# A fused attention and quantised-MLP block on one core: both batches' attention steps issued in one piece

## The reference

```python
x = x + fake_quant(layernorm(x)) @ fake_quant(ctx)          # ctx 2 x 2048 x 2048, 8-bit steps
x = x + attention(layernorm(x), Wq, Wkv, Wo)                # 32 heads of 64, one shared key/value head
x = x + layernorm(x) @ W4 + bias                            # W4: 4-bit weights, scales per 128 rows

# attention: q = h @ Wq; k, v = split(h @ Wkv)
scores = einsum('bqhd,bkd->bhqk', q, k) / 8 + slope[h] * (k_pos - q_pos), masked above the diagonal
out = einsum('bhqk,bkd->bqhd', softmax(scores), v) @ Wo
```

## Time and profile before

| | us |
|---|---|
| median of 3 runs | 397.14 (396.98 to 397.20) |
| profiled execution | 397.71 |
| its span in the trace | 395.9 |
| TensorE busy | 354.6 (90%) |
| VectorE busy | 328.7 (83%) |
| ScalarE busy | 221.7 (56%) |

### The profile page before, as it was taken

The page is one execution under the profiler, slowest core; times in us unless marked ns, Lnnn a source line. Parts: engine busy times, 40 slices in busy tenths (PEclk is TensorE's granted clock), DMA queues, the critical chain, the costliest instruction groups (busy, mean ns, idle before and its releaser), DMA issues.

```text
span 395.9 us, 5717 instructions
## 1 busy us (share of the span) xinstructions
PE 354.6 (90%) x2342; PEld 265.2 (67%) x2342; DVE 328.7 (83%) x333; ACT 221.7 (56%) x316; POOL 29.8 (8%) x69
## 2 busy tenths in 40 slices
PE   0076865899999999999999999999999999999996
PEld 0022231425888787888877888888888788888884
DVE  1689889797879898884999967888988999999924
ACT  1788988997515872845856570742834923333100
POOL 6000000006590000000011000000000000000000
PEclk9999889699999999999999999999999999999999
DMA  8999999999055487496539624786000020000006
GB/s 333 422 436 424 428 434 427 427 397 395 17 212 170 152 208 218 118 216 208 206 111 269 208 99 165 260 309 223 2 0 1 2 106 2 0 0 2 0 0 212
DMA packets 21958, 77.37 MB, mean 195 GB/s; under 512 B 1354, under 2 KB 1402, under 8 KB 18810
## 3 DMA queue, kind: packets, MB, share of 16 engines
q1 hardware_dynamic: 21924, 77.01, 53.5%
q10 hardware_dynamic: 8, 0.00, 0.0%
HBM read 74.91 MB, written 2.10 MB: 194 GB/s over the span
## 4 chain that ended last, share of the span: by engine, by line
PE 72%; DVE 19%; DMA 4%; issue 3%; ACT 1%; ACTq 0%; DVEq 0%
PE bank L1189 22%; PE bank L1049 11%; PE bank L1050 11%; PE bank L1051 11%; DVE q L708 7%; PE bank L1010 4%; DMA raw<-in_L_attn_Wq 3%; PE bank L1062 2%; DVE stats L622 2%; PE bank L1042 2%; PE bank L1134 2%; DMA prm_row<-in_L_xattn_x_zp 2%; PE bank L1072 1%; PE bank L1153 1%; DVE resid L720 1%
## 5 line engine op out<-in xcount | busy, mean ns | idle before, releaser
L486 ACT ACTIVATE w_hi<-raw 128x2048 fp32r<-128x2048 f32 x29 | 55.2, 1912 | 44.3 <-DMA raw<-in_L_attn_Wo 22.6
L652 DVE TENSOR_TENSOR w_lo<-raw,w_hi 128x2048 fp32r<-128x2048 f32 x27 | 62.6, 2326 | 12.7 <-ACT w_hi L486 12.7
L1189 PE MATMUL bank<-w_hi,hd 128*128 128x512 f32 x208 | 53.2, 391 | 0.1
L1010 PE MATMUL bank<-q,at 128*128 128x512 bf16 x128 | 38.4, 429 | 16.1 <-DVE q L708 15.5
L1189 PEld LDWEIGHTS bank<-w_hi,hd 128*128 128x128 f32 x208 | 38.8, 188 | 8.5 <-issue 0.5
L708 DVE TENSOR_SCALAR q<-q 128x2048 bf16<-128x2048 uint8 x32 | 38.4, 1218 | 4.7 <-PE bank L1017 4.3
L1049 PE MATMUL bank<-w_hi,hd 128*128 128x512 f32 x104 | 40.7, 391 | 0.0
L1050 PE MATMUL bank<-w_lo,hd 128*128 128x512 f32 x104 | 40.5, 389 | 0.0
L1051 PE MATMUL bank<-w_hi,hd 128*128 128x512 f32 x104 | 40.5, 389 | 0.0
L1049 PE MATMUL bank<-w_hi,xt 128*128 128x512 f32 x96 | 38.9, 405 | 0.0
L1050 PE MATMUL bank<-w_lo,xt 128*128 128x512 f32 x96 | 37.5, 390 | 0.0
(11 more groups left out here) (158 smaller groups left out, 616.7 us busy)
## 6 DMA issues: line engine op xcount, KB each, us to landing
raw<-in_ctx SPq DMA_DIRECT2D x8, 2048.0 KB, 15.3
raw<-in_L_attn_Wq SPq DMA_DIRECT2D x16, 1024.0 KB, 6.0
ctx_more<-in_ctx SPq DMA_DIRECT2D x7, 2048.0 KB, 16.1
raw<-in_L_attn_Wo SPq DMA_DIRECT2D x13, 1024.0 KB, 5.1
raw_fifth<-in_L_attn_Wo SPq DMA_DIRECT2D x3, 1024.0 KB, 5.1
resid<-in_x SPq DMA_DIRECT2D x2, 1024.0 KB, 12.6
ctx_more<-in_ctx SPq DMA_DIRECT2D x2, 1024.0 KB, 15.3
scale<-in_L_ffn_scales SPq DMA_DIRECT2D x16, 128.0 KB, 6.7
```

What stands on the lines that cost most here:

```text
L486: nc.scalar.activation(hi_slots[s], raw_slots[s], ACT.Copy).then_inc(w_hi_set, 1)
L652: nc.vector.tensor_tensor(lo_slots[s], raw_slots[s], hi_slots[s].bitcast(F32), ALU.subtract).then_inc(w_lo_set, 1)
L1010: mm(bank[:, 4 * b + n, :], at[:, k, b * P:(b + 1) * P], q16[:, i % 2, n * CH:(n + 1) * CH], start=start, stop=False)
L1189: return mm(bank[:, 4 * b + n, :], left[:, j, b * P:(b + 1) * P], right[slot_of(W_F + j)][:, n * CH:(n + 1) * CH], start=part == 0 and j = ...
```

## The change

1. The scores of both batches of a group are made in one piece, `scores(g)`, in all 512 columns of banks 4 to 7. It waits for the query transpositions of both batches. It stands where the first batch's scores stood.
2. `attend(g)` makes the heads of both batches in one piece, in columns 0 to 255 of the same banks, over scores that VectorE has read. It stands where the second batch's piece stood.
3. `heads_hi(g)` and `heads_lo(g)` split both batches' output in one instruction each, of twice the width.
4. ScalarE does the exponentials of both batches one behind the other, and then the upper parts of the next two weight pieces. VectorE does both batches' biased scores and maxima, then one remainder, then both batches' divisions and transpositions, then two remainders.
5. The values go out of PSUM by one copy into `v_rows`; `v_rep` is made from it by 8 copies on VectorE and 8 on ScalarE. ScalarE's piece 6 and its 8 copies come before the loading of the exponential's table.
6. `o_granule(5, 0)` comes before `o_granule(3, 0)`.

```diff
+        v_rows = sb("v_rows", [P, B, DH], F32)
...
-            return bank[:, BLOCK_BANK:BLOCK_BANK + 4, (2 + b) * P:(3 + b) * P]
+        HEADS_AT = bank[:, BLOCK_BANK:BLOCK_BANK + 4, 0:B * P]
...
+            def heads_hi(g):
+                act.wait_ge(av_done, g + 1)
+                nc.scalar.activation(hd_hi[:, 4 * g:4 * g + 4, :], HEADS_AT, ACT.Copy).then_inc(hi_out, B)
...
+            upper_w(6)
+            act.wait_ge(v_out, 1)
+            for j in range(4):
+                for i in range(2, 4):
+                    nc.scalar.activation(v_rep[BLK * i:BLK * i + BLK, :, j, :], v_rows[BLK * j:BLK * j + BLK],
+                                         ACT.Copy).then_inc(v_dup_act, 1)
             nc.scalar.activation(warm[:], eps_col[:], ACT.Exp)
-            upper_w(6)
...
                 upper_w(4 * n + 3)
                 exps(ua)
+                exps(ub)
                 upper_w(4 * n + 4)
-                exps(ub)
-                heads_hi(ua)
                 upper_w(4 * n + 5)
-                heads_hi(ub)
+                heads_hi(n - 1)
...
-                    dve.wait_ge(score_done, u - 1)
+                    dve.wait_ge(score_done, n)
...
+            nc.vector.tensor_copy(v_rows[:], bank[:, KV_BANK, B * P:B * P + B * DH].rearrange("p (b d) -> p b d", b=B)
+                                  ).then_inc(v_out, 1)
+            q_blocks(1)
+            dve.wait_ge(v_out, 1)
             for j in range(4):
-                for i in range(4):
+                for i in range(2):
...
-                dve.wait_ge(score_done, u + 1)
+                dve.wait_ge(score_done, u // B + 1)
...
-                    dve.wait_ge(av_done, u - 1)
+                    dve.wait_ge(av_done, u // B)
...
+            def heads_lo(g):
+                dve.wait_ge(hi_out, 4 * B + B * (g + 1))
+                nc.vector.tensor_tensor(hd_lo[:, 4 * g:4 * g + 4, :], HEADS_AT, hd_hi[:, 4 * g:4 * g + 4, :].bitcast(F32),
+                                        ALU.subtract).then_inc(lo_out, B)
...
-                remainder_w(4 * n + 3)
                 biased_scores(ub)
                 maxima(ub)
+                remainder_w(4 * n + 3)
                 over_sum(ua)
                 prob_blocks(ua)
-                remainder_w(4 * n + 4)
                 over_sum(ub)
                 prob_blocks(ub)
-                heads_lo(ua)
+                remainder_w(4 * n + 4)
                 remainder_w(4 * n + 5)
-                heads_lo(ub)
+                heads_lo(n - 1)
...
+            def scores(g):
+                pe.wait_ge(qt_set, B * (g + 1))
+                if g == 0:
+                    pe.wait_ge(v_out, 1)
+                    pe.wait_ge(k_dup, 8)
                 else:
+                    pe.wait_ge(lo_out, 4 * B + B * g)
+                for b in range(B):
...
+            def attend(g):
+                if g == 0:
+                    pe.wait_ge(v_dup, 8)
+                    pe.wait_ge(v_dup_act, 8)
+                pe.wait_ge(score_out, B * (g + 1))
+                for b in range(B):
+                    probs = prob_t[:, b, :].rearrange("p (e i j q) -> p e j i q", e=2, i=4, j=4)
+                    pe.wait_ge(prob_t_set, B * g + b + 1)
...
                 if n >= 2:
-                    scores(ua)
+                    scores(n - 1)
                 q_granule(w, 1)
                 if n == 1:
-                    scores(ua)
+                    scores(n - 1)
                 q_granule(w + 1, 0)
-                scores(ub)
                 q_granule(w + 1, 1)
                 q_granule(w + 2, 0)
                 q_granule(w + 2, 1)
-                attend(ua)
                 q_granule(w + 3, 0)
                 if n >= 2:
-                    attend(ub)
+                    attend(n - 1)
                 q_granule(w + 3, 1)
                 if n == 1:
-                    attend(ub)
+                    attend(n - 1)
...
             o_granule(4, 0)
-            attend(7)
+            attend(3)
             o_granule(4, 1)
+            o_granule(5, 0)
             o_granule(3, 0)
-            o_granule(5, 0)
             o_granule(3, 1)
```

More of the change, by code:

```diff
@@ L197, in perceiver @@
         v_dup = sem("v_dup")
+        v_dup_act = sem("v_dup_act")
+        v_out = sem("v_out")
         stored = sem("stored")
@@ L276, in perceiver @@
         O_BANK = ((0, 1), (2, 3), (0, 1), (6, 7))
-        def heads_at(b):
-            return bank[:, BLOCK_BANK:BLOCK_BANK + 4, (2 + b) * P:(3 + b) * P]
+        HEADS_AT = bank[:, BLOCK_BANK:BLOCK_BANK + 4, 0:B * P]
         def tr_bank(n, g):
@@ L806, in _ @@
             dve.wait_ge(vt_done, 1)
-            values = bank[:, KV_BANK, B * P:B * P + B * DH].rearrange("p (b d) -> p b d", b=B)
+            nc.vector.tensor_copy(v_rows[:], bank[:, KV_BANK, B * P:B * P + B * DH].rearrange("p (b d) -> p b d", b=B)
+                                  ).then_inc(v_out, 1)
+            q_blocks(1)
+            dve.wait_ge(v_out, 1)
             for j in range(4):
-                for i in range(4):
+                for i in range(2):
                     nc.vector.tensor_copy(v_rep[BLK * i:BLK * i + BLK, :, j, :],
-                                          values[BLK * j:BLK * j + BLK]).then_inc(v_dup, 1)
-            q_blocks(1)
+                                          v_rows[BLK * j:BLK * j + BLK]).then_inc(v_dup, 1)
             def lower_scales(h):
@@ L829, in biased_scores @@
                                                          scalar=slope[:, u // B, e:e + 1],
-                                                         in1=bank[:, BLOCK_BANK:BLOCK_BANK + 4, e * P:(e + 1) * P],
+                                                         in1=bank[:, BLOCK_BANK:BLOCK_BANK + 4,
+                                                                  (2 * (u % B) + e) * P:(2 * (u % B) + e + 1) * P],
                                                          op0=ALU.mult, op1=ALU.add)
@@ L1115, in value_rows @@
                 ins.then_inc(vt_done, 1)
[L1117 to L1124, removed]
+            def scores(g):
+                pe.wait_ge(qt_set, B * (g + 1))
+                if g == 0:
+                    pe.wait_ge(v_out, 1)
                     pe.wait_ge(k_dup, 8)
                 else:
[L1127 to L1135, removed]
-                ins.then_inc(score_done, 1)
@@ new lines, in scores @@
+                for b in range(B):
+                    heads = qt[:, b, :].rearrange("p (e c m) -> p e c m", e=2, c=2)
+                    for e in range(2):
+                        for c in range(2):
+                            for i in range(4):
+                                rows = slice(BLK * i, BLK * i + BLK)
+                                ins = mm(bank[:, BLOCK_BANK + i, (2 * b + e) * P:(2 * b + e + 1) * P], heads[rows, e, c],
+                                         k_rep[rows, b, c, :], start=c == 0, stop=c == 1)
@@ new lines, in scores @@
+                ins.then_inc(score_done, 1)
+            def attend(g):
[6 more added lines that the diff above has]
+                    pe.wait_ge(prob_t_set, B * g + b + 1)
+                    for j in range(4):
+                        for e in range(2):
+                            for r in range(4):
+                                rows = slice(BLK * r, BLK * r + BLK)
+                                ins = mm(bank[e * DH:(e + 1) * DH, BLOCK_BANK + r, b * P + BLK * j:(b + 1) * P],
+                                         v_rep[rows, b, j, :], probs[rows, e, j, j:], start=j == 0, stop=j == 3)
@@ L1282, in _ @@
                 q_granule(w + 2, 1)
-                attend(ua)
                 q_granule(w + 3, 0)
                 if n >= 2:
-                    attend(ub)
+                    attend(n - 1)
                 q_granule(w + 3, 1)
                 if n == 1:
-                    attend(ub)
+                    attend(n - 1)
             o_granule(0, 0)
-            scores(6)
+            scores(3)
             o_granule(0, 1)
             o_granule(1, 0)
-            scores(7)
             o_granule(1, 1)
@@ L1299, in _ @@
             o_granule(2, 1)
-            attend(6)
             o_granule(4, 0)
-            attend(7)
+            attend(3)
             o_granule(4, 1)
+            o_granule(5, 0)
             o_granule(3, 0)
-            o_granule(5, 0)
             o_granule(3, 1)
```

## The result

| | before | after |
|---|---|---|
| median, us (5 runs each) | 397.14 (396.87 to 397.20) | 394.95 (394.89 to 395.11) |
| profiled execution, us | 397.71 | 394.95 |
| its span, us | 395.9 | 393.1 |
| from the first query granule of round 1 to the product behind the last `attend` | 104.80 | 102.27 |

The ratio is 0.9947 (95% interval 0.9932 to 0.9961), 2.2 us less. The profiled execution of before was 0.6 us above its median, that of after is the median, so the two traces differ by 2.8. Of these, 0.26 lie ahead of the attention: the first query granule starts at 125.60 before and 125.34 after, with no edit there (in the eleven traces of the changed kernel and its variants this start lies between 125.23 and 125.82, so 0.26 is within what executions differ by).

The account below looks back on a forecast made before the run. TensorE bounds the kernel from about 126 us. Six merges x 0.37 = 2.2, plus 0.32 wait, less 0.07: about 2.5 us off 397.71, 395.2; that execution being 0.6 above median, 394.7. Range 393.9 to 396.8.

Parts of the forecast that it names:

- The bound: From about 126 us to the end TensorE sets the time; work moved on VectorE or ScalarE alone is worth nothing.
- A merge: Second batch's scores or attend following in the same TensorE pass saves 0.37 or 0.36 us; eight merges.
- edges-only rival: Each merge on TensorE saves only the 0.21 us seen at piece edges: 1.2 us less, 396.0; chance 0.18.
- rival of no saving: A merge saves nothing because each batch fills anew: 0.5 us more, 397.6; chance 0.08.
- The new wait: Round 1, second scores: TensorE waits some 0.8 us for both batches' remainders and query transpositions, with one granule as cover.
- 0.04 to the subtraction: Round 1, chain to the second scores: 0.04 us from ScalarE's copy to VectorE's heads subtraction.
- The old wait: Round 3: TensorE's 0.32 us wait for `hd_lo` ahead of the second attention product goes.
- Margins of round 1: VectorE's roundings and probabilities in round 1 are all in time for TensorE, by 0.7 to 1.5 us.
- Value copies: Before round 1's first scores and exponentials: the split copies on VectorE and ScalarE cost nothing, being covered by TensorE's work.
- Round 3: Probabilities, hanging on weight 14's landing at 182.9, ready at 199.7; TensorE at `attend(2)` at 200.2, 0.5 us in hand.
- slower rival: Round 3: weight 14 landing after 184.2 delays TensorE at `attend(2)`; 6 us late gives 399.4; chance 0.07.
- Behind the attention: VectorE's chain after the attention moves along with TensorE; if it stayed put it would take back 0.5 us.

Follow-up runs that it names:

- the cut pieces: Changed kernel with seven of eight merged pieces cut in two by three full-size products of the following granule; 398.32 us, ratio 1.0026 to the kernel before.
- the version with the queries first: Changed kernel, but in round 1 VectorE transposes both batches' queries before it splits the heads; 393.91 us, ratio 0.9915 to the kernel before.

## Why the prediction was right

The forecast was 394.7, in a range of 393.9 to 396.8; 394.95 is 0.25 off. Not all terms were as good as their sum, and that it came so close is in part luck, as follows.

- **The bound.** TensorE from 126 us on: right. As far as the runs can tell, every kernel above moved its time by what its TensorE pieces and waits moved, and work moved on ScalarE alone (exponentials) did nothing.
- **A merge**, 0.37: the account gives 0.42, and so does a cut. For the second batch 0.93 and 0.80 were forecast, 0.90 and 0.79 measured (64 times the forecast's own 0.0124 is 0.79, not 0.80). The price of a single piece was short as well: I took 0.228 us per product from one row of 24, whose first takes longer; the products of the next passes start 0.227 apart (96 of them from 326.58 to 348.35), and with that a single `scores` is 1.32, not 1.30, and an `attend` 1.19, not 1.16. Over eight merges this was 0.4 us too little gain. The edges-only rival (0.21) and the rival of no saving are refuted by the cut pieces. The Trainium skill's estimate from "TensorE: Matmul & The Clock Gate", Single matmul latency (two fixed parts of 166 ns, which the page gives for a lone bf16 product; 0.33 us a merge), is in the right direction and 0.09 short of what was measured. That a change of mode drains the array (the Trainium skill, "TensorEngine Tiling (Array Packing)", Key Properties) fits with the cuts; these do not tell a drain from other costs of entering.
- **The new wait**, 0.8 us ahead of the second `scores`: right in place, cause and order of size; it measured 1.22. The step that failed is "0.04 to the subtraction": it was 0.47. ScalarE started 0.07 later than the sum had it, and TensorE 0.09 earlier. The terms of that sum also add up to 3.76, not the 3.72 that it gives; measured was 4.17. The two misses, 0.4 too little gain and 0.4 too little wait, have nothing to do with each other and cancel by luck.
- **The old wait**, 0.32: gone, worth 0.38.
- **Margins of round 1.** Forecast: rounding 6 at 138.2 with 0.7 in hand. It ended at 138.0, with TensorE there at 138.6; the cut pieces used that margin up, and the wait appeared. The probabilities of b were forecast for 148.3, and were ready at 148.05.
- **Value copies**: no cost, right. The prediction gave them no gain either, but behind merged `scores` the old copies would have cost 0.30 (the experiment's trace), so point 5 of the change is what kept that term out of the sum. VectorE's eight took 1.91 us, 0.24 each from SBUF, against 0.32 from PSUM; ScalarE's took 2.63, 0.33 each. ScalarE came to the exponentials at 135.8, just when the maxima did.
- **Round 3**: probabilities forecast for 199.7 and TensorE for 200.2; it was 198.9 and 199.9. The landing of weight 14 was 0.8 us earlier (ScalarE starts on it at 182.07, not 182.91), so 1.0 was in hand. The slower rival had the chain right, and was that far off. It took the landing as independent of TensorE, and in the version with the queries first it was not.
- **Behind the attention**: nothing lost, as forecast. The swap in round 4, which the prediction calls needed, was not: undone, it costs nothing, with 0.34 us left where 0.4 was forecast.
- **The profiled execution against the median.** I took 2.45 off both. The traces differ by 2.8 and the medians by 2.2; in the stage it is 2.53. Of the 0.6 us between them, 0.26 lie ahead of the attention, and the rest stays open: there is one trace of before, so the 2.53 of the stage, and with it the 0.42 of a merge, rest on one execution. The cut pieces give 0.42 as well.

## What to carry to other kernels

A short piece of small products between large ones costs its entry, filling and exit each time, here 0.42 us out of 1.2 to 1.3, so two that stand in the queue of a full TensorE are worth merging; but merging also joins their conditions, so work out for each merged piece the chain from the last thing that frees it to the last thing that it waits for, and compare it with the work that lies between. Where that chain is longer than the cover, either take what is ready early out of its end (the query transpositions here) or move the piece one granule on. Where TensorE is the bound, reordering on the other engines pays only at such a place.

## What the runs showed that was not expected

On VectorE, an instruction that waits for ScalarE started 0.47 us after its releaser's end in one place of the list, in seven traces out of seven, and 0.10 with one more instruction or seven more ahead of it, in four out of four; in rounds 2 and 4 of the changed kernel it was 0.09. A load of instructions moved with it, and whether that is the cause is not shown. On a path that sets the end this is worth 0.37 us, a sixth of what the whole change brought. It hid the cost of another edit: the old value copies make the first `scores` 0.30 us late and the time does not move (394.98 against 394.95). Two medians that agree to 0.03 us, closer than their runs do among themselves, held two opposite effects of 0.3 us, and only the trace told them apart.
